# High halves of the routed weights by a rounding transfer straight into the ring

## What is computed

```
h = h + attention(layernorm(h))
x = layernorm(h)
shared = gelu(x @ shared_up[0]) @ shared_down[0]            # 256 -> 1024 -> 256
probs = softmax(x @ router_w); two largest of 8 per token
routed = sum over the two: gate * (gelu(x @ up[e]) @ down[e])
h = h + (shared + routed + x)
```

## Time and profile before

| | before |
|---|---|
| median of 3 runs | 359.08 us (358.6 to 359.09) |
| the profiled execution | 360.22 us |
| its span, first to last instruction | 358.4 us |
| PE busy | 309.5 us (86%) |
| GpSimd (POOL) busy | 203.3 us (57%) |
| VectorE (DVE) busy | 160.0 us (45%) |
| ScalarE (ACT) busy | 152.5 us (43%) |
| moved by DMA | 39.39 MB |

### The profile page before, as it was taken

How to read it: one execution, slowest core, us unless ns; L and a number is a source line. 1 busy time by engine, 2 the same in 40 slices (tenths; PEclk the granted TensorE clock), 3 DMA queues, 4 the chain that set the end, 5 groups by cost and what they waited for, 6 DMA issues and landing times.

```text
span 358.4 us, 6664 instructions
## 1 busy us (share of the span) xinstructions
PE 309.5 (86%) x2063; PEld 275.4 (77%) x2064; DVE 160.0 (45%) x398; ACT 152.5 (43%) x327; POOL 203.3 (57%) x155
## 2 busy tenths in 40 slices
PE   1778387899857897999989999999999999999970
PEld 1556246898737697899968998998998998998970
DVE  3244656888835264966414332332332332332320
ACT  2364431457676582435234433433433433434310
POOL 1242110843866300046598889889988889535651
PEclk9969769899985999999999999999999999999998
DMA  7934101031345433016635336523455433333522
GB/s 253 284 119 156 33 15 38 2 117 37 87 136 182 140 98 103 2 59 215 227 112 190 118 136 190 175 89 116 161 146 161 142 49 59 44 44 44 59 31 29
DMA packets 21357, 39.39 MB, mean 110 GB/s; under 512 B 2855, under 2 KB 17658, under 8 KB 19034
## 3 DMA queue, kind: packets, MB, share of 16 engines
q0 software_dynamic: 7392, 25.43, 26.5%
q1 hardware_dynamic: 13658, 13.51, 12.0%
q10 hardware_dynamic: 288, 0.20, 0.2%
HBM read 28.32 MB, written 6.93 MB: 98 GB/s over the span
## 4 chain that ended last, share of the span: by engine, by line
PE 42%; POOL 13%; DVE 12%; issue 12%; DMA 11%; ACT 3%; POOLq 3%; SPq 1%; DVEq 0%
DMA out_tokens<-xy_all,dest 10%; PE ps L898 8%; PE ps L900 8%; PE ps L899 8%; PE ps L949 7%; POOL ring L397 6%; PE ps L777 5%; PE ps L805 3%; POOL ring L396 3%; POOL out_tokens L517 2%; POOLq L514 2%; PE ps L869 2%; DVE h L1186 1%; PE ps L1012 1%; DVE st L1194 1%
## 5 line engine op out<-in xcount | busy, mean ns | idle before, releaser
L397 POOL TENSOR_TENSOR ring<-stage,ring 128x512 fp32r<-128x512 f32 (+2 forms) x30 | 76.1, 2536 | 2.5
L1439 DVE TENSOR_TENSOR hgT<-ps,hgT 128x512 fp32r<-128x512 f32 x50 | 32.2, 686 | 72.3 <-ACT hgT L767 72.3
L898 PE MATMUL ps<-ring,hgT 128*128 x200 | 58.0, 290 | 2.1 <-DVE xy_all L1445 1.5
L900 PE MATMUL ps<-ring,hgT 128*128 x200 | 55.9, 279 | 0.0
L899 PE MATMUL ps<-ring,hgT 128*128 x200 | 55.9, 279 | 0.0
L517 POOL DMA_INDIRECT out_tokens<-xy_all,dest x25 | 39.5, 1581 | 27.6 <-DMA out_tokens<-xy_all,dest 15.4
L759 ACT ACTIVATE hg<-ps 128x512 f32<-128x512 f32 x50 | 29.9, 599 | 47.7 <-PE ps L900 47.7
L507 POOL DMA_INDIRECT xy_all<-normalized_tokens,dest x25 | 24.9, 995 | 43.0 <-DVE dest L1401 35.7
L898 PE MATMUL ps<-ring,xgT 128*128 x100 | 41.3, 413 | 1.1 <-issue 0.6
L396 POOL TENSOR_SCALAR ring<-stage 128x512 fp32r<-128x512 f32 (+2 forms) x30 | 38.5, 1283 | 2.7 <-PEq L1026 2.5
L898 PEld LDWEIGHTS ps<-ring,hgT 128*128 128x128 f32 x200 | 37.6, 188 | 2.6 <-issue 2.6
(11 more groups left out here) (182 smaller groups left out, 602.2 us busy)
## 6 DMA issues: line engine op xcount, KB each, us to landing
stage<-in_w_up POOLq DMA_DIRECT2D x9, 1024.0 KB, 5.4
stage<-in_w_dn POOLq DMA_DIRECT2D x9, 1024.0 KB, 5.5
xg<-xy_all SPq DMA_DIRECT2D x25, 128.0 KB, 2.0
xp<-in_patches SPq DMA_DIRECT2D x4, 384.0 KB, 5.4
normalized_tokens<-hn SPq DMA_DIRECT2D x4, 276.0 KB
residual_tokens<-h SPq DMA_DIRECT2D x4, 276.0 KB
ring<-in_tok_w SPq DMA_DIRECT2D x1, 768.0 KB, 6.1
base<-residual_tokens SPq DMA_DIRECT2D x2, 384.0 KB, 3.6
```

Of the source, the lines that this page charges most:

```text
L397: return nc.gpsimd.tensor_tensor(lo, stage[:, part, c0:c1], hi.bitcast(F32), ALU.subtract)
L898: nc.tensor.matmul(o, a[0], b[0], start=n == 0, stop=False)
L900: last = nc.tensor.matmul(o, a[1], b[0], start=False, stop=n == len(pairs) - 1)
L1439: v.tensor_tensor(hgT[:, c, 1, 4 * half:4 * half + 4, :], ps[:, turned_bank + half, :].rearrange("p (k t) -> p k t", k=4), hgT[:, c, 0, 4 ...
```

## The change

The high halves of sets 3 to 8 are no longer made by GpSimd. A new step `open_slot` waits until the slot is free and then issues two transfers, `up` and `down`, from memory straight into the slot's `hi` copy. Since `ring` is of the rounded type and the memory is not, the transfer rounds. The loads into `stage` stay as they are, so sets 3 to 8 are read from memory twice. `prepare_half` keeps the subtraction alone, which waits for both transfers. Sets 0 to 2 are made as before. The list of GpSimd's steps is rearranged, so that each slot is opened well ahead of its subtractions.

```
+        high_in = [sem(f"high_in{i}") for i in range(4)]
...
-            def prepare_half(x, part, c0=0, c1=UPW):
-
-                if x > RING and part == 0 and c0 == 0:
+            def open_slot(x):
+
+                if x > RING:
 
                     pool.wait_ge(ffn_done, tiles_before(x - RING) + 1)
                     pool.sem_inc(slot_free, 1)
-                elif x in (RING - 1, RING) and part == 0:
+                else:
 
                     pool.wait_ge(ffn_done, 1)
-                last = split(x, part, c0, c1)
+                for part in range(2):
+                    pool.dma_start(ring[:, x % RING, 0, UPW * part:UPW * (part + 1)],
+                                   (w_up, w_dn)[part][x, :, :]).then_inc(high_in[2 * (x % 2) + part], 16)
+
+            def prepare_half(x, part, c0=0, c1=UPW):
+
+                pool.wait_ge(w_in[part], 16 * (x + 1))
+                pool.wait_ge(high_in[2 * (x % 2) + part], 16 * ((x - RING + 1) // 2 + 1))
+                hi, lo = (ring[:, x % RING, v, UPW * part + c0:UPW * part + c1] for v in range(2))
+                last = nc.gpsimd.tensor_tensor(lo, stage[:, part, c0:c1], hi.bitcast(F32), ALU.subtract)
                 if c1 < UPW:
                     return
...
             gather_rows(10, FREE_ROWS)
+            open_slot(3)
+            pool.wait_ge(base_out, 16 * (NSG + 1))
+            pool.wait_ge(r_additions, 1)
...
+            gather_rows(13, 15)
+            open_slot(4)
             prepare_half(3, 0)
             prepare_half(3, 1)
...
```

More of the change, by code:

```diff
@@ L529, in _ @@
             gather_rows(10, FREE_ROWS)
-            prepare_half(3, 0)
-            prepare_half(3, 1)
+            open_slot(3)
             pool.wait_ge(base_out, 16 * (NSG + 1))
@@ L538, in _ @@
             gather_rows(13, 15)
+            open_slot(4)
+            prepare_half(3, 0)
+            prepare_half(3, 1)
+            gather_rows(15, 17)
             prepare_half(4, 0)
-            gather_rows(15, 17)
+            gather_rows(17, 19)
             prepare_half(4, 1)
-            gather_rows(17, 19)
             add_rows(0, 1)
-            prepare_half(5, 0)
+            open_slot(5)
             gather_rows(19, 21)
             add_rows(1, 2)
+            prepare_half(5, 0)
+            gather_rows(21, 23)
             prepare_half(5, 1)
-            gather_rows(21, 23)
             add_rows(2, 3)
+            open_slot(6)
+            gather_rows(23, 25)
             prepare_half(6, 0)
-            gather_rows(23, 25)
             prepare_half(6, 1)
-            add_rows(3, 4)
+            open_slot(7)
+            add_rows(3, 5)
             prepare_half(7, 0)
-            add_rows(4, 5)
             prepare_half(7, 1)
-            add_rows(5, 6)
+            open_slot(8)
+            add_rows(5, 7)
             prepare_half(8, 0, 0, UPW // 2)
-            add_rows(6, 8)
+            add_rows(7, 8)
             prepare_half(8, 0, UPW // 2, UPW)
```

## The result

The changed kernel takes **368.51 us** (median of 4, 365.98 to 370.1) against 359.08 (the kernel before was run once more beside it, in 362.28 us; its median stays). The profiled executions say 368.23 against 360.22, spans 366.4 and 358.4, so the two traces to compare differ by 8.0 us.

The account below looks back on a forecast made before the run. PE was taken to pace the routed experts at 6.68 us a tile, with tile 2's copy on the path; 4.9 + 1.7 = +6.6 us, 366.8 by the profiled execution, less 1.14: 365.7 us (359.0 to 371.5).

Parts of the forecast that it names:

- The entry's traffic: Routed stage's entry: two 1 MB transfers delay tile 2's copy from 182.69 to 187.6 us, +4.9 us.
- The clock: After the entry's PE gap: granted clock falls for 3.4 us, +1.7 us; 0 without a fall, 5.1 if 10.2 us.
- POOL's relief: Routed experts: 28.6 us of POOL work removed, all under PE's work, so 0 us.
- the steps: Routed tiles after the entry: steps of 6.68 us again, no wait for a slot.
- Order: GpSimd's rearranged list: slot 5 ready in time with 5 us of room, no term; +1 us if issues cost 1.6.
- tail: Last stores: store 11 comes some 3.6 us earlier against PE, so the tail stays, 0 us.
- the count's third and fourth terms: Count to slot 5: slot 4 with gathers and reloads 16.5 us; stores 0 and 1, gathers and slot 5 21.9 us.
- the later pairs of transfers: Copies into xg after the entry: delayed up to 9.7 us of the 13.4 available, so hidden.
- The end: From the last store to the end of the span: the prediction gave no term.
- Slow rounding: Rival: rounding transfers need 6.7 us each instead of 2.7, entry +12.8 us, 373.6 us (halfway 371.1); chance 0.18.
- the rule that the queues take turns: Rival at the entry: SP's stores and copy served between the transfers, copy at 185.7, 362.1 to 363.8 us; chance 0.2.
- Not slower: Rival at the entry: transfers start moving only after base stores and copy are through, 359.1 us; chance 0.1.

Follow-up runs that it names:

- The dose series: Changed kernel with one or four transfers at the entry instead of two: 365.93 us (ratio 1.0189) with one, 372.16 us (ratio 1.0375) with four.
- the plain loads: Kernel before with two plain 1 MB loads that nothing reads added on GpSimd's queue at the entry: 367.71 us, ratio 1.0203.
- the first experiment: Changed kernel with slot 3 opened only after the base stores and the gathers of tiles 13 and 14: 363.69 us, ratio 1.015.
- the copies moved: Kernel before with the copies of tiles 2 and 3 into xg ahead of SyncE's last base stores: 357.78 us, ratio 0.996.

## Why the prediction was right

Forecast 365.7 us (359.0 to 371.5), slower; measured 368.51.

- **The entry's traffic** (+4.9 us): +5.44 in the trace. The landing of tile 2 was forecast for 187.6 and came at 187.46; the entry had been reached 0.67 us earlier, which makes the rest. The dose series and the plain loads show that it is traffic. That the landing fits so closely is in part luck: the 0.6 us between the last transfer and the copy were a choice between 0.3 and 1.4, and the runs show that this distance is no constant. The copy landed 1.3 us behind one transfer, 0.5 behind two, and 0.8 ahead of the last of four.
- **The clock** (+1.7 us): it fell, and stayed for 10.2 us instead of 3.4. It cost 2.29 us and not the 5.1 of that bound, since 4.3 us of the low stretch passed while PE was idle anyway (183.2 to 187.5). Half of the 5.9 us that were left would be 2.95, but from the transposes of tile 2 to the first product it took 1.06 us (1.07 before), and only the twelve products behind lost time, 5.15 us for 2.84.
- **POOL's relief** (0) and **the steps** (0): right, 155.79 us against 155.82.
- **Order** (slot 5 with 5 us of room, tail 0): right for this kernel. Slot 5 was ready at 236.25 + 4.60 = 240.85, 53.3 us behind the wait for the base stores where 53.8 were counted, and PE did not wait. (By the prices stated beside them the count's third and fourth terms are 16.2 and 20.9 and not 16.5 and 21.9; the measured 53.3 hold two waits for landings, 0.6 and 1.4 us, that the count had not.) But the count had POOL gain 3.6 us against PE; with PE itself 7.7 us late, measured from the entry (179.2 us to the scaling of the last tile for 171.5), and the list 5.0 us longer, it was 2.7. The step missed two waits of GpSimd behind its own transfers, 5.0 us in all for the landing of high halves and 7.3 for store 5. I had priced the later pairs of transfers for SyncE's copies only; in GpSimd's own queue they stand behind a reload and landed after a median of 7.3 and 9.4 us between 200 and 340 us. That the tail stayed 0 all the same is luck: the late PE hid the longer list. In the first experiment, where PE is on time, the same step is worth 3.3 us.
- **The end** (nothing): +0.97 us, not foreseen; see below.
- **The rivals.** Slow rounding is out: 5.5 and 8.3 us to landing, like plain loads, at 363 to 430 GB/s. Of the rule that the queues take turns (the Trainium skill, "DMA: Bandwidth & Descriptors", section "Queues, rings and completion order") the run with four transfers agrees with the turns (the copy landed ahead of a transfer that had been issued before it), and no run with the time I had drawn from them: in the changed kernel the base store was not through between the transfers but landed with the second, at 178.82 + 8.1 = 186.9, and the copy at 187.46 and not at 185.7. "Not slower" would have needed a late start of the transfers; they moved 1 MB within 5.5 us. The lower end of the forecast's own spread was mis-stated: with the stores between and no fall of the clock its terms give 359.08 + 4.6 = 363.6 and not 362.6; the range does not hang on it.

The sum of the terms is 6.6 us, the spans differ by 8.0, the medians by 9.4 (interval 5.5 to 11.5). What lies between 8.0 and 9.4 is not resolved by these runs.

## What to carry to other kernels

Taking work from an engine that is 57% busy gains nothing where another engine never waits for it; ask first who waits. What replaces the work lands somewhere: look at which small transfers are on the path at the very time the new large ones are issued, on whatever queue, and move the small ones ahead. And where an engine issues both large loads and small transfers whose landing it waits for, each load ahead of them in its queue is time on its own list, so work taken out of such a list can come back as waits.

## What was not expected of the hardware

- **Rounding in the transfer is free.** 1 MB from f32 to the rounded form landed after 5.5 us at the entry, a plain MB at the same place after 5.7.
- **A small copy beside large loads.** 128 KB (rows of 1 KB) landed after 2.0 us alone, 5.8 with one, 7.6 with two and 11.9 with four transfers of 1 MB (rows of 8 KB) issued around it.
- **The end of the program.** From the start of the last store to the end of the span it is 7.43 us in the kernel before, 7.4 with the copies moved, 7.6 with two more loads or transfers on GpSimd's queue, and 8.4 in every kernel with the twelve transfers. That the number of transfers issued on its queue makes the difference was not tried by itself.
